# Graph attention on one core: window sums on VectorE, head 0's score rows by products, and a new order of splits and loads

## Reference

```python
# edges (src, dst), 20000 of them, sorted by dst; edge_weight for each
x1 = relu(layernorm(x) @ W_ah + b_ah)
for W, a_src, a_dst, b in three layers:          # 4 heads of C = 192
    h = (x1 @ W).reshape(N, 4, 192)
    e = leaky_relu((h * a_src).sum(-1)[src] + (h * a_dst).sum(-1)[dst], 0.2)
    p = exp(e - segment_max(e, dst)[dst])
    out = segment_sum(p / segment_sum(p, dst)[dst] * h[src], dst) + b
    xs.append(relu(out))
x = x + relu(concat(xs) @ W_out + b_out)
# then a mixture of experts, two graph convolutions with edge_weight, attention and a feed-forward block
```

## Time and profile before

| | us |
|---|---|
| median of 3 runs | 3148.31 (3144.77 to 3156.2) |
| the profiled execution | 3156.52 |
| its span, first to last instruction | 3154.8 |
| TensorE, VectorE, ScalarE, GpSimd busy | 2602.8, 1977.4, 1386.1, 356.7 |
| mean granted TensorE clock | 0.900 of 2.4 GHz |

### The profile page before, as it was taken

The page is one execution under the profiler, slowest core; times in us unless marked ns, Lnnn a source line. Parts: engine busy times, 40 slices in busy tenths (PEclk is TensorE's granted clock), DMA queues, the critical chain, the costliest instruction groups (busy, mean ns, idle before and its releaser), DMA issues. The chain is left out here.

```text
span 3154.8 us, 40044 instructions
## 1 busy us (share of the span) xinstructions
PE 2602.8 (83%) x14620; PEld 2311.3 (73%) x14621; DVE 1977.4 (63%) x2803; ACT 1386.1 (44%) x2313; POOL 356.7 (11%) x309
## 2 busy tenths in 40 slices
PE   5774888887986977975899689789897998999876
PEld 5763778887986977973888557367665776999766
DVE  7886287777867853345655343542895556989654
ACT  0343267775865831110566410031796103777330
POOL 1351040040030000001233210000000000111000
PEclk9986988998998988996999869879998997999978
DMA  0012101111111253221899750124561222444304
GB/s 33 20 41 67 62 10 62 53 41 51 52 43 43 70 135 80 44 64 57 264 251 256 186 127 0 49 88 150 139 130 37 83 64 51 107 93 86 92 1 103
DMA packets 107250, 267.13 MB, mean 85 GB/s; under 512 B 11062, under 2 KB 49448, under 8 KB 106090
## 3 DMA queue, kind: packets, MB, share of 16 engines
q1 hardware_dynamic: 99474, 238.26, 27.9%
q0 software_dynamic: 7616, 26.74, 3.9%
HBM read 194.41 MB, written 66.73 MB: 83 GB/s over the span
## 5 line engine op out<-in xcount | busy, mean ns | idle before, releaser
L902 PE MATMUL ps<-h,e_gat_aggregate 125*125 125x193 f32 x2400 | 404.9, 332 | 52.5 <-DVE e_gat_aggregate L884 52.5
L902 PEld LDWEIGHTS ps<-h,e_gat_aggregate 125*125 125x125 f32 x2400 | 398.7, 191 | 58.7 <-DVE e_gat_aggregate L884 58.7
L882 DVE TENSOR_TENSOR e_gat_aggregate<-e_gat_aggregate 125x1250 f32<-125x1250 f32 x120 | 174.7, 1456 | 77.9 <-ACT e_gat_aggregate L853 74.7
L103 PE MATMUL ps<-gat_w_pair_gat_scores,x_turned 128*125 128x384 f32 x1080 | 195.7, 344 | 32.1 <-DVE gat_w_pair_gat_scores L749 32.1
L103 PE MATMUL ps<-w_pair_dense_rows_from,col_dense_rows_from 128*125 128x384 f32 x1080 | 208.8, 351 | 16.2 <-DVE w_pair_dense_rows_from L1075 13.4
L103 PEld LDWEIGHTS ps<-gat_w_pair_gat_scores,x_turned 128*125 128x125 f32 x1080 | 194.5, 190 | 33.1 <-DVE gat_w_pair_gat_scores L749 32.9
L103 PEld LDWEIGHTS ps<-w_pair_dense_rows_from,col_dense_rows_from 128*125 128x125 f32 x1080 | 195.9, 194 | 17.9 <-issue 14.7
L850 ACT ACTIVATE e_gat_aggregate<-row_gat_aggregate,from_src 125x1250 f32<-125x1250 f32 x120 | 161.7, 1347 | 87.6 <-PE ps L902 62.5
L2437 DVE TENSOR_TENSOR ln_home<-p_attend,p_high_attend 125x1254 fp32r<-125x1254 f32 x120 | 182.7, 1535 | 26.9 <-ACT p_high_attend L2423 24.1
L2415 ACT ACTIVATE p_attend<-ps 125x1254 f32<-125x1254 f32 (+2 forms) x168 | 148.7, 915 | 79.6 <-PE ps L2378 77.7
L1930 DVE TENSOR_SCALAR_CACHE_REDUCE res_attention_statistics<-ps 125x1250 f32<-125x1250 f32 x120 | 173.0, 1459 | 12.7 <-PE ps L1907 7.4
(11 more groups left out here) (387 smaller groups left out, 5189.9 us busy)
## 6 DMA issues: line engine op xcount, KB each, us to landing
stock<-in_moe_w SPq DMA_DIRECT2D x34, 1152.0 KB, 7.0
row_gat_aggregate<-r_scratch SPq DMA_DIRECT2D x24, 625.0 KB, 6.1
V_home<-q_scratch SPq DMA_DIRECT2D x44, 312.5 KB, 6.3
ln_home<-q_scratch SPq DMA_DIRECT2D x36, 312.5 KB
ln_home<-k_scratch SPq DMA_DIRECT2D x36, 312.5 KB
rows_dense_rows_from<-node_scratch SPq DMA_DIRECT2D x8, 1080.0 KB
q_scratch<-V_home SPq DMA_DIRECT2D x6, 1250.0 KB, 4.6
k_scratch<-V_home SPq DMA_DIRECT2D x6, 1250.0 KB, 4.8
```

The lines of the kernel that those rows point to most:

```text
L103: last = pe.matmul(out, left(x), right(y), start=start and n == 0, stop=stop and n == 2)
L882: v.tensor_tensor(e[:, n % 3, 0, :], e[:, n % 3, 0, :], e[:, n % 3, 1, :], ALU.max).then_inc(p_step, 1)
L902: last = pe.matmul(ps[0:TP, bank(head, d // 2), d % 2 * (C + 1):(d % 2 + 1) * (C + 1)], e[:, n % 3, 0, d * TP:(d + 1) * TP], h[:, t, head, :],
```

## The change

Three phases change. **build_adjacency**: ScalarE writes part 0 of the sums to `count` itself, and parts 1 to 3 to `stage`. The two adds move from GpSimd to VectorE, where they stand among the first destinations of the window after the next: so `adj` is padded by two windows in front, GpSimd clears `stage` at the start, and the last two windows are added after the loop. **gat_scores and gat_aggregate**: after the transposes TensorE makes 20 products of a column of z, repeated over 125 columns, with the identity; each puts 125 values of a score row on all partitions. In gat_aggregate ScalarE and VectorE copy these rows out of PSUM to the buffer of head 0. SyncE no longer loads head 0 and waits for the store only before the rows of head 1. **dense_rows_from**: splits of weights 0 to 2 come first, the row tile of tile 2 is loaded after weight block 12 and not after x, and its turning goes among the last openings of tile 1.

```diff
...
     dests = ph.sb("destination_iota", [TP, NPAD])
-    stage = ph.sb("window_sums", [TP, 2, NT, 4, WIN])
+    stage = ph.sb("window_sums", [TP, 2, NT, 3, WIN])
...
     first_hot = ph.sb("first_hot", [TP, 2, 4, WIN], BF16)
-    adj = ph.sb("adjacency", [TP, NT, NPAD])
...
+    LAG = 2
+    adj = ph.sb("adjacency", [TP, NT, NPAD + LAG * WIN])
...
         "first_ready0", "first_ready1", "first_free0", "first_free1",
-        "staged", "ahead_in", "pool_sum", "window_out", "adj_stored")}
+        "staged", "ahead_in", "parts_sum", "stage_clear", "window_out", "adj_stored")}
...
                 here = slice(first * WIN, min((first + STORE) * WIN, N))
-                move_rows(sp, rows_out[:, :, here], adj[:, :, here], s["adj_stored"])
+                there = slice(here.start + LAG * WIN, here.stop + LAG * WIN)
+                move_rows(sp, rows_out[:, :, here], adj[:, :, there], s["adj_stored"])
...
             pool.memset(ones[:], 1.0)
+            pool.memset(stage[:], 0.0)
...
-            with pool.Fori(0, NWIN // 2) as i:
-                for odd in range(2):
-                    w = 2 * i + odd
-                    pool.wait_ge(s["staged"], w + 3)
-                    here = bass.ds(w * WIN, WIN)
-                    pool.tensor_copy(count[:, :, here], stage[:, odd, :, 0, :])
-                    pool.tensor_tensor(stage[:, odd, :, 1, :], stage[:, odd, :, 1, :], stage[:, odd, :, 2, :],
-                                       ALU.add).then_inc(s["pool_sum"], 1)
-                    pool.wait_ge(s["pool_sum"], w + 1)
-                    pool.tensor_tensor(adj[:, :, here], stage[:, odd, :, 1, :], stage[:, odd, :, 3, :],
-                                       ALU.add).then_inc(s["window_out"], 1)
...
+            def parts_sum(odd, w):
...
+                v.wait_ge(s["staged"], w + 1)
+                v.tensor_tensor(stage[:, odd, :, 0, :], stage[:, odd, :, 0, :], stage[:, odd, :, 1, :], ALU.add).then_inc(s["parts_sum"], 1)
...
+            def adjacency(odd, w):
...
+                v.wait_ge(s["parts_sum"], w + 1)
+                v.tensor_tensor(adj[:, :, bass.ds(w * WIN, WIN)], stage[:, odd, :, 0, :], stage[:, odd, :, 2, :],
+                                ALU.add).then_inc(s["window_out"], 1)
...
                         dst_of(first_hot, j, bass.ds(first, 1), w).then_inc(first_ready[j], 1)
+                        if j == 0:
+                            parts_sum(odd, w)
+                    adjacency(odd, w)
...
                             dst_of(dst_hot, j, bass.ds(c, 1), w).then_inc(hot_ready[j], 1)
-            v.wait_ge(s["window_out"], NWIN + 2)
+            for odd in range(LAG):
+                parts_sum(odd, NWIN + odd)
+                adjacency(odd, NWIN + odd)
...
             pe.sem_inc(s["staged"], 2)
-            pe.sem_inc(s["window_out"], 2)
...
                         n = 4 if b < 2 else 2
-                        last = a.activation(stage[:, odd, 4 * b:4 * b + n].rearrange("p t k d -> p (t k d)"),
-                                            ps[0:TP, 3 * odd + b, 0:n * 128], ACT.Copy)
+                        sums = ps[0:TP, 3 * odd + b, 0:n * 128].rearrange("p (t k d) -> p t k d", k=4, d=WIN)
+                        a.activation(stage[:, odd, 4 * b:4 * b + n], sums[:, :, 1:4, :], ACT.Copy)
+                        last = a.activation(count[:, 4 * b:4 * b + n, bass.ds(w * WIN, WIN)], sums[:, :, 0, :], ACT.Copy)
...
+def first_row(ps, k, t):
...
+    return ps[0:TP, 5 - 3 * k + t // 4, t % 4 * TP:(t % 4 + 1) * TP]
...
     a_in, h_sum, h_out, v_step, ones_in = ph.sem("a_in"), ph.sem("h_sum"), ph.sem("h_out"), ph.sem("v_step"), ph.sem("ones_in")
-    peak_ready, peak_turned, peak_read, r_ready, r_turned, r_out, r_stored = (
-        ph.sem("peak_ready"), ph.sem("peak_turned"), ph.sem("peak_read"), ph.sem("r_ready"), ph.sem("r_turned"),
-        ph.sem("r_out"), ph.sem("r_stored"))
+    peak_ready, peak_turned, peak_read, r_ready, r_turned, r_out = (
+        ph.sem("peak_ready"), ph.sem("peak_turned"), ph.sem("peak_read"), ph.sem("r_ready"), ph.sem("r_turned"), ph.sem("r_out"))
...
             for k in range(2):
-                sp.dma_start(r_scratch[k].rearrange("h (t n) -> (h t) n", n=TP), rows[:, k, :]).then_inc(r_stored, 16)
-            sp.wait_ge(r_stored, 32)
+                sp.dma_start(r_scratch[k].rearrange("h (t n) -> (h t) n", n=TP), rows[:, k, :]).then_inc(g["r_stored"], 16)
...
             last.then_inc(r_turned, 1)
+            for k in range(2):
+                for t in range(NT):
+                    last = pe.matmul(first_row(ps, k, t), z[:, k, t:t + 1].broadcast_to([TP, TP]), ident[0:TP, 0:TP], start=True, stop=True)
+            last.then_inc(g["row_there"], 1)
...
     ph = Phase(nc, g, "gat_aggregate")
+    ph.sems += [g["r_stored"], g["row_there"]]
+    row_copied = ph.sem("row_copied")
...
                     sp.dma_start(row[:, head % 2, k, :], r_scratch[k, head:head + 1, :].partition_broadcast(128)).then_inc(row_in[head % 2][k], 16)
-            load_rows(0)
+            sp.wait_ge(g["r_stored"], 32)
...
+        def first_pieces(k):
...
+            whole = ps[0:TP, 5 - 3 * k:7 - 3 * k, 0:4 * TP], row[0:TP, 0, k, 0:8 * TP].rearrange("p (b c) -> p b c", c=4 * TP)
+            return whole, (ps[0:TP, 7 - 3 * k, 0:2 * TP], row[0:TP, 0, k, 8 * TP:N])
...
         def _(a):
+            a.wait_ge(g["row_there"], 1)
+            for piece, to in first_pieces(1):
+                a.activation(to, piece, ACT.Copy).then_inc(row_copied, 1)
...
                         a.wait_ge(p_used, n - 2)
-                    if t == 0:
-                        a.wait_ge(row_in[head % 2][0], 16 * (head // 2 + 1))
+                    if t == 0 and head == 0:
+                        a.wait_ge(row_copied, 4)
+                    elif t == 0:
+                        a.wait_ge(row_in[head % 2][0], 16 * ((head + 1) // 2))
                     a.activation(e[:, n % 3, 0, :], row[0:TP, head % 2, 0, :], ACT.Exp, bias=from_src[:, head, t:t + 1])
-                    if t == 0:
-                        a.wait_ge(row_in[head % 2][1], 16 * (head // 2 + 1))
+                    if t == 0 and head >= 1:
+                        a.wait_ge(row_in[head % 2][1], 16 * ((head + 1) // 2))
...
             step = Chain(v, v_step)
+            v.wait_ge(g["row_there"], 1)
+            for piece, to in first_pieces(0):
+                v.tensor_copy(to, piece).then_inc(row_copied, 1)
...
             sp.wait_ge(turned, OLD // 512)
-            for k in range(KEPT, KD):
+            for k in range(KEPT, kt):
+                if k >= KD:
+                    sp.wait_ge(w_split, k - KD + 1)
                 load_weights(k)
-            for k in range(KD, kt):
-                sp.wait_ge(w_split, k - KD + 1)
-                load_weights(k)
+                if k == late:
+                    sp.wait_ge(turned, groups)
+                    move_rows(sp, rows, source[2 * TP:3 * TP, :], row_in)
...
             move_rows(sp, x, x_in.rearrange("(t p) d -> p t d", p=TP), x_loaded)
-            for t in range(2, NT):
+            for t in range(3, NT):
...
                 opening(1, k)
-            for k in range(KD, kt):
+            for k in range(KD, late):
...
                 opening(1, k)
-            for q in range(groups):
-                turn(2, q)
+            for k in range(late, kt):
+                opening(0, k)
+            for k in range(late, kt):
+                opening(1, k)
+                if k - late < groups:
+                    turn(2, k - late)
...
-            high(0, 0, 1, 2)
             weights(0, 1, 2)
-            high(0, 3)
+            high(0, 0, 1)
             weights(3)
-            high(0, 4)
+            high(0, 2, 3, 4)
...
+            weights(0, 1, 2)
...
             low(0, 1)
-            weights(0)
+            weights(3)
             low(0, 2)
-            weights(1)
             move(0, 3)
-            weights(2)
+            move(0, 4)
             low(0, 3)
-            move(0, 4)
-            weights(3)
+            move(1, 0)
             low(0, 4)
-            move(1, 0)
...
         g["y_added"] = ctx.enter_context(nc.semaphore("y_added"))
+        g["r_stored"], g["row_there"] = (ctx.enter_context(nc.semaphore(name)) for name in ("r_stored", "row_there"))
```

## The result

The changed kernel takes 3138.03 us in the median of 20 runs (3132.43 to 3145.79), the kernel before 3151.95 us in 20 runs on the same chips (3143.58 to 3159.68): a ratio of 0.9959, 95% interval 0.9951 to 0.9966, or 12.9 us less. Forecast were 28.4 us less. The profiled execution took 3135.3 us with a span of 3133.5. Its difference to the profile before, 21 us, is more than the change took: up to the stage behind dense_rows_from it is 12.7 us (ScalarE, ACT in the rows, loads a table at 1399.98 before, at 1387.28 after), and what comes later is code that the change doesn't touch.

A forecast was written before the change was run, and what follows sets the result against it. No engine was taken as busy throughout: stages follow one another, each bound by its own chain, with VectorE pacing build_adjacency. Terms of -21.4, -2 and -5 us sum to -28.4, from 3148.3 to 3120 us, range 3106 to 3140.

The forecast's parts named there:

- part A: Window sums in build_adjacency, casts and adds taken off GpSimd: -21.4 us, bounds about -4 to -29.
- The first term: VectorE in build_adjacency: 43.7 us of stretch removed less 32 us for 80 adds, net 11.7 us less work.
- The 5.8 us of holes ahead of src_hot: VectorE's idle time before src_hot in build_adjacency, put down to the sequencer; the second add would run in it: 5.8 us.
- The 9 us out of the wait for TensorE: Of VectorE's 17.3 us standing for TensorE before src_hot, 9 us would take the new adds.
- The pauses that come back: Sequencer pauses at every second window of build_adjacency, covered by the stretch before, would return: 5 us.
- The adds waited 1.2 us in the loop for ScalarE, put at nothing: In build_adjacency, adds wait for ScalarE's copy of two windows before; its three more copies a window were costed at nothing.
- The ends: Start and finish of build_adjacency: clearing the sums buffer adds 1.6 us, the tail after the last product loses 1.5.
- Part B: First head's score rows made by TensorE products in three layers: -2 us in all, bounds -8 and +6.
- rival (2): Score-row products run at the half clock with the stage's end behind them: +6 instead of -2, 3128 us; chance 0.15.
- the clock rule: TensorE after idling works at 1.2 GHz until busy again; by this alone the score-row products give +6 us.
- Part C: dense_rows_from, weight splits first and the row tile ahead of x: -5 us, bounds -7 and +1.
- Rival (1): VectorE stays the bound in build_adjacency, adds cost 0.5 us beside nothing: sum -11, 3137 us; chance 0.13.

The follow-up runs named there:

- e9: Kernel of e5 with VectorE also waiting for its own first add ahead of the window's steps: 3146.44 us, ratio 0.9976.
- e5: Changed kernel with VectorE's first add behind both first_hot of a window and the second behind the window's steps: 3116.24 us, ratio 0.9885.
- e6: Changed kernel with the clearing of the sums buffer moved behind the signal that starts TensorE: 3134.36 us, ratio 0.9942.
- e2: Kernel before with only the changes of gat_scores and gat_aggregate: 0.9995 of before, 1.6 us less.
- e1: Kernel before with only the change of build_adjacency: 0.9995 of before, 1.6 us less.
- e3: Kernel before with only the change of dense_rows_from: 0.9981 of before, 6.0 us less.
- e8: Changed kernel with VectorE waiting for x only ahead of the first sum with x, not the columns of tile 2: 3129.02 us, ratio 0.9930.
- e10: Kernel of e8 with x loaded in two parts and row tile 3 between them: 3122.58 us, ratio 0.9906.
- e7: Kernel before with ScalarE writing the counts from PSUM and GpSimd keeping its two adds: 3150.51 us, ratio 0.9993.
- e11: Changed kernel with 12 transposes of the identity, into a bank nobody reads, in TensorE's idle time before z: 3134.64 us, ratio 0.9945.

## Why the prediction was wrong

**The step that failed** is in part A: "The stretch shrinks by 11.7 + 5.8 + 9 - 5 = 21.5 us." The loop shrank by 6.7 us (231.1 to 224.4). The first term held: without idle time the loop is 189.3 us before and 178.4 after, 10.9 less. The other three, -9.8 together, came out as +4.2: idle time in the loop went from 41.8 to 46.0 us. Term by term:

- The 5.8 us of holes ahead of src_hot, which the second add was to fill, became 8.2, since that add waits for the first, and the inner loop's entry comes only behind this wait. e9 shows it with the wait added, e5 with the wait not ahead of the entry (1.0). This missed by 8.2 us.
- The 9 us out of the wait for TensorE were 1.9. The trace before would have told: 15.7 of the 17.3 us stand between two steps of a window, and only 1.6 between first_hot and src_hot, where the adds were put. This missed by 7.1 us; that the place is the reason is read from the trace, and no run tests it.
- The pauses that come back, put at 5 us, were 2.6 (idle time ahead of first_hot, 20.0 to 22.6: issue rose by 9.2, and 6.6 of waits for TensorE that lay at the same places went). This was 2.4 us better than forecast.
- The adds waited 1.2 us in the loop for ScalarE, put at nothing.

Together 2.4 - 1.9 + 2.6 + 1.2 = 4.3. I had taken idle time in the queue of the kernel before for time that a new instruction could use. But an instruction that brings a wait of its own ahead of a loop's entry adds to the idle time for issue, and a wait is of use only to an instruction that stands at its place.

The ends held: the clear cost 1.65 us (forecast 1.6, and e6 takes it back whole), and the tail from the last dst_hot to the last store fell from 5.40 to 3.93 us (forecast 1.5 less). Adds of 0.48 us, 0.40 of a place, were as forecast.

**Part B** was forecast at -2 us and gave +0.2, +0.6 and -1.2, which is -0.4, in the profiles; e2's median is too coarse to tell this from -2. The price of the products was between the two ends, 6.17 and 6.16 us in the mixed layers and 4.53 in the third, where 5.3 was the full clock's. The stage's end does wait for them, and took 2.15 us where 1.6 was forecast. Of rival (2), half clock with the end behind, the end held in all three layers and the clock only in part: 0.72 and 0.73 in the first two, which gave +0.2 and +0.6 where it said +2.1. The +6 us by the clock rule took it that a pause of 2.6 us lowers the clock; layer 3 shows that it does not by itself.

**Part C** was forecast at -5 us, and the stage became 4.9 us shorter. The steps: opening(0, 0) at 5.6 us for 8.4 (2.8 sooner, as forecast), the long run 6.6 us sooner for 5.7, x 2.35 for 1.1, TensorE going on with tile 2 at 72.0 where 73.4 was forecast and 78.3 stood before. Of these 6.2 us the rest of the stage gave 1.3 back (193.3 for 192.0 us). A single trace of this stage is good to a few us only (under e1), so that both numbers are 5 is partly luck; e3's median gives 6.0 us (3.2 to 8.8). What I didn't see is that the wait for x ahead of the columns is needless there; e8 and e10 find 14.7 us behind it, three times what the change took.

**The sum** from the traces is -6.5 - 0.4 - 4.9 = -11.8 us, beside the measured -12.9. Rival (1), "gives the gain back", had the right size at -11, by half its mechanism: the adds did not cost the 0.5 us a place that it said, but the idle time that was to take them did not.

## What to carry to other kernels

Before you fill an engine's idle time, ask what its sequencer does in it: a wait placed ahead of a loop's entry or turn holds back the bookkeeping behind it, and costs far more than the wait. Put dependent instructions apart, with the second one last before the loop turns. Where that engine is the bound, count one place per instruction in full unless a row shows idle time at the very place where it will stand. When one load is moved ahead, look for who waits for the load it was moved past, and whether that wait must stand so early.

## What the runs showed of the hardware

A wait of VectorE for its own last instruction, ahead of a hardware loop's entry, cost 0.76 us of idle time each time (30.4 us in 40 windows), though the same kind of wait ahead of a plain instruction let it start 0.19 us behind. VectorE's instructions are stretched beside GpSimd's adds of two inputs (dst_hot 0.34 to 0.94 us); without GpSimd's cast the stretch was 40.3 us for 43.7 (e7, which also changes ScalarE's copies). After a TensorE pause of 2.58 us the granted clock was 0.72 in layer 1, where the transposes before it had run at 0.55 (near the lower level, 1.2 GHz), and 1.00 (2.4 GHz) in layer 3, whose last ten transposes had run at 1.00, in 0.13 us each. The Trainium skill (TensorE: Matmul & The Clock Gate, What's actually happening) says that the default state is throttled and that activity releases it; the trace agrees where 12 transposes in the pause brought the products of layers 1 and 2 to 1.00 (e11), and layer 3 shows that a pause of 2.58 us alone did not lower the clock.
